# Two attentions and two layers of experts in one kernel: row buffers of the first experts, their places, and the order of keys and values

## The reference

```python
x = x + tanh(g_xattn[0]) * attention0(layernorm(x), ctx, ctx)     # 16 heads of 16, 128 keys per batch
x = x + tanh(g_ffn[0])   * experts0(layernorm(x))                 # 8 experts, top 2 of each token, 256 -> 1024 -> 256, exact GELU
x = x + tanh(g_xattn[1]) * attention1(layernorm(x), ctx, ctx, bias)
x = x + tanh(g_ffn[1])   * slots_and_experts1(layernorm(x))       # 16 slots, 16 experts with SiLU gates, attention back
```

## Time and profile before

| | us |
|---|---|
| median of 3 runs | 1462.82 (1461.97 to 1466.13) |
| the profiled execution | 1461.18 |
| its span, first to last instruction | 1459.4 |
| granted TensorE clock, mean | 0.978 |
| busy: PE, DVE, ScalarE, POOL | 1359.3, 928.2, 759.3, 381.4 |

### The profile page before, as it was taken

How to read it: one execution, slowest core, us unless ns; L and a number is a source line. 1 busy time by engine, 2 the same in 40 slices (tenths; PEclk the granted TensorE clock), 3 DMA queues, 4 the chain that set the end, 5 groups by cost and what they waited for, 6 DMA issues and landing times.

```text
span 1459.4 us, 39417 instructions
## 1 busy us (share of the span) xinstructions
PE 1359.3 (93%) x14238; PEld 1167.0 (80%) x14238; DVE 928.2 (64%) x2579; ACT 759.3 (52%) x1731; POOL 381.4 (26%) x478
## 2 busy tenths in 40 slices
PE   6999999995889999999999996999999999899798
PEld 5888888884779898989889995889989898645476
DVE  4789999886445455545445544788888887412187
ACT  3666666652545455555455552555656655332344
POOL 0244444443011303021321004433433431100131
PEclk9999999998899999999999997999999999999999
DMA  4665445454121212121221102631111110299911
GB/s 158 240 239 171 150 160 171 154 182 155 63 88 37 95 44 96 37 95 47 85 95 40 42 30 69 220 130 45 47 59 46 45 52 13 115 388 429 352 53 66
DMA packets 94567, 175.18 MB, mean 120 GB/s; under 512 B 9008, under 2 KB 84784, under 8 KB 89904
## 3 DMA queue, kind: packets, MB, share of 16 engines
q1 hardware_dynamic: 87376, 143.30, 27.4%
q0 software_dynamic: 7008, 29.37, 5.8%
HBM read 112.87 MB, written 59.77 MB: 118 GB/s over the span
## 4 chain that ended last, share of the span: by engine, by line
PE 74%; DVE 14%; DMA 7%; issue 3%; ACT 2%; POOL 0%; SPq 0%; DVEq 0%; ACTq 0%; PEldq 0%; POOLq 0%
PE ps L1222 13%; PE ps L1207 6%; PE psS L511 4%; DMA arena<-xs_rows 4%; PE psS L1207 4%; PE ps L663 3%; PE psT L1207 3%; PE ps L554 3%; PE psT L520 3%; PE ps L558 3%; DVE arena L879 3%; PE ps L618 2%; PE ps L603 2%; PE ps L630 2%; PE ps L1194 2%
## 5 line engine op out<-in xcount | busy, mean ns | idle before, releaser
L520 PE MATMUL psT<-arena 32*128 32x128 f32 x2048 | 148.8, 283 | 0.1
L511 PE MATMUL psS<-arena 32*128 32x256 f32 x1024 | 140.3, 392 | 0.7 <-ACT arena L756 0.7
L1253 ACT ACTIVATE arena<-arena 128x512 f32<-128x512 f32 x142 | 89.7, 632 | 96.1 <-DVE arena L1279 96.1
L1222 PE MATMUL ps<-ring_hi,hT_hi 128*128 x568 | 139.1, 283 | 0.5 <-ACT hT_hi L1235 0.5
L1222 PE MATMUL ps<-ring_lo,hT_hi 128*128 x568 | 139.3, 283 | 0.0
L1298 DVE TENSOR_TENSOR arena<-ps,arena 128x256 f32<-128x256 f32 x71 | 30.2, 425 | 152.9 <-PE ps L1222 152.9
L520 PEld LDWEIGHTS psT<-arena 32*128 32x128 f32 x2048 | 124.3, 186 | 1.2 <-issue 1.2
L1222 PEld LDWEIGHTS ps<-ring_hi,hT_hi 128*128 128x128 f32 x568 | 108.6, 191 | 3.5 <-issue 0.7
L1222 PEld LDWEIGHTS ps<-ring_lo,hT_hi 128*128 128x128 f32 x568 | 108.8, 192 | 2.8
L879 DVE TENSOR_REDUCE arena<-psS 128x8 f32<-128x1024 f32 x64 | 78.4, 1225 | 47.4 <-PE psS L511 47.4
L1235 ACT CAST hT_hi<-psT 128x512 fp32r<-128x512 f32 x71 | 41.7, 587 | 127.0 <-PE psT L1194 126.9
(11 more groups left out here) (288 smaller groups left out, 3720.1 us busy)
## 6 DMA issues: line engine op xcount, KB each, us to landing
arena<-wset_dram SPq DMA_DIRECT2D x24, 2048.0 KB, 15.2
xs_rows<-arena SPq DMA_DIRECT2D x32, 1024.0 KB, 5.7
arena<-w_dram POOLq DMA_DIRECT2D x6, 2048.0 KB, 9.0
arena<-xs_rows SPq DMA_DIRECT2D x71, 128.0 KB, 2.0
ys_rows<-arena SPq DMA_DIRECT2D x71, 128.0 KB, 1.7
arena<-ctxT_dram SPq DMA_DIRECT2D x64, 128.0 KB, 2.2
x_all<-x_dram SPq DMA_DIRECT2D x32, 128.0 KB, 2.1
arena<-w_dram SPq DMA_DIRECT2D x2, 2048.0 KB, 11.7
```

What stands on the lines that cost most here:

```text
L511: last = nc.tensor.matmul(psS[:, b, c * D:(c + 1) * D], qT[p, k % 3, c, :], kbd[p, k % 3, c, :, :], start=A, stop=A or c == 1, skip_group_ ...
L520: nc.tensor.matmul(psT[:, b, j * P:(j + 1) * P], kbd[p, (k - 1) % 3, c, par, :], qT[p, (k - 1) % 3, c, :], start=j == 0, stop=False, skip_ ...
L1222: last = nc.tensor.matmul(ps[5][:, 0:D], hp[:, f, :], wp[:, bass.ds(ring[j - 1], 1), o:o + D], start=n == 0 and f == 0 and wp is ring_hi, ...
L1253: nc.scalar.activation(v, v, ACT.Gelu).then_inc(ge_a.sem, 1)
```

## The change

1. `xs`, the buffers of a unit's rows, become four (`XS`), and lie in the first two weights of layer 0, which are dead by then but for the small product `prep`; SP issues `rows_in(j + 4)` where it issued `rows_in(j + 2)`. A unit's output is stored to the rows of `xs_dram` that it came from, through a second read of `unit_s`; `ys_dram` is gone, and so is the table of places. Units beyond the last real one get seven spare blocks, zeroed at the start of the kernel. The scatter's index is kept for the later gather, one column for each batch.
2. The weights of the two experts are made by `weights(dve, j)` in iterations 3, 4 and 5, in front of the wait for the unit's last product.
3. Unit 0 is always expert 0's first block; its rows are loaded before the unit table is there. PE starts a unit's products when the high part is there, waits for the low part in front of the third pair, and transposes unit 1 between the halves of unit 0, into bank 5. b1 is loaded in two halves. `prep` uses banks 6 and 7, and its DVE part comes one step later.
4. Attention 0 makes keys and values of batch 0 ahead of the steps (banks 6 and 7), of batches 1 and 2 behind the queries of batch 0 (banks 3 and 2). Attention 1 makes those of batches 0 to 4 ahead of the steps (banks 6, 7, 3, 2, 4), with two more context buffers and two more of `kbd` and `vz`. SP loads the contexts 2 and 3 during `moe0`, and 4 and 5 at the head of attention 1; its steps load a context only from batch 6 on.
5. ScalarE runs one exponential of one column at the head of each attention, which brings its table.

```diff
+XS = 4
-ROWS_EACH = TOKENS + P
+ROWS_EACH = TOKENS
+SPARE = E0 - 1
...
+        xs = w_sb[:, 0:2].rearrange("p n c d -> p (n c d)").rearrange("p (n d) -> p n d", n=XS)
...
             def sync(sp):
+                for i in () if A else (4, 5):
+                    sp.wait_ge(kv_p.sem, kv_p.at(i - 4, "V"))
+                    sp.dma_start(ctxT[:, i % 2].rearrange("p c t -> p (c t)"), a["ctxT"][i]).then_inc(ld_ctx[i % 2], 16)
                 for k in steps:
...
+                    if not A and k == 2 + EARLY_SETS:
+                        sp.wait_ge(av_p.sem, av_p.at(4, "av"))
                     if not A and 3 <= k < 3 + EARLY_SETS:
                         sp.dma_start(set_at(k - 3).rearrange("p e f -> p (e f)"), a["wset"][k - 3]).then_inc(ld_set[k - 3], 16)
...
-                    if valid(k + 3) and k + 3 >= 2:
+                    if valid(k + 3) and k + 3 >= (2 if A else 6):
                         i = k + 3
-                        before(sp, pre_p.sem, pre_p.at(k + 1, "V"))
+                        before(sp, kv_p.sem, kv_p.at(k + 1, "V"))
                         sp.dma_start(ctxT[:, i % 2].rearrange("p c t -> p (c t)"), a["ctxT"][i]).then_inc(ld_ctx[i % 2], 16)
...
                 if A:
                     pe.wait_ge(ld_first, 32)
                     pe.wait_ge(ld_kv, 16)
+                    keys(0, 6)
+                    values(0, 7)
                 else:
                     pe.wait_ge(ld_w, 16)
+                    for i in range(early):
+                        keys(i, early_bank[i])
+                        values(i, early_bank[i])
...
-                    if valid(k + 1):
-                        pe.wait_ge(ld_ctx[(k + 1) % 2], dma_at(k + 1, (k + 1) % 2))
+                    if valid(k + 1) and k + 1 >= early:
                         before(pe, m_a.sem, m_a.at(k - 1, "mT"))
                         before(pe, pre_a.sem, pre_a.at(k, "Q"))
...
+                        keys(k + 1, 6)
+                        values(k + 1, 6)
...
+                    if A and k == -1:
+                        for i in range(1, early):
+                            keys(i, early_bank[i])
+                            values(i, early_bank[i])
...
             def scalar(act):
...
                 if A:
+                    act.wait_ge(setup_v, 2)
+                    nc.scalar.activation(table[:, :], ones[:, 0:1], ACT.Exp)
                     act.wait_ge(setup_v, 3)
+                    act.wait_ge(kv_p.sem, kv_p.at(0, "K"))
+                    keys(0, 6)
+                else:
+                    nc.scalar.activation(table[:, :], ones[:, 0:1], ACT.Exp)
+                    for i in range(early - 1):
+                        act.wait_ge(kv_p.sem, kv_p.at(i, "V"))
+                        keys(i, early_bank[i])
+                        values(i, early_bank[i])
...
-                        before(dve, scat[sl_i % 2], dma_at(sl_i - 2, sl_i % 2, 2) if valid(sl_i - 2) else 0)
-                        nc.vector.tensor_copy(idx_put[:, sl_i % 2, :], slot_f[:, :, sl_i]).then_inc(rk_v.sem, 1)
+                        nc.vector.tensor_copy(slot_i[:, :, sl_i], slot_f[:, :]).then_inc(rk_v.sem, 1)
...
-                    if A and k == B + 2:
+                    if A and k == B + 3:
                         dve.wait_ge(prep_p, 1)
...
-                sp.wait_ge(route_v.sem, route_v.at(0, "unit_e"))
                 for s in scat:
                     sp.wait_ge(s, 16 * B)
                 sp.wait_ge(zero_dump, 16)
-                rows_in(0)
-                rows_in(1)
+                sp.wait_ge(prep_p, 1)
+                sp.dma_start(xs[:, 0, :], xs_dram[0:P, :]).then_inc(ld_xs[0], 16)
+                sp.wait_ge(route_v.sem, route_v.at(0, "unit_e"))
+                sp.wait_ge(prep_p, 3)
+                for j in range(1, XS):
+                    rows_in(j)
+                sp.dma_start(b1_sb[:, E0 // 2:].rearrange("p e f -> p (e f)"), a["b1"][:, E0 // 2 * F0:].partition_broadcast(P))\
+                    .then_inc(ld_b1[1], 16)
                 sp.dma_start(b2_sb.rearrange("p e d -> p (e d)"), a["b2"].partition_broadcast(P)).then_inc(ld_b2, 16)
+                for i in range(2):
+                    sp.dma_start(ctx_more[:, i].rearrange("p c t -> p (c t)"), a["ctxT"][2 + i]).then_inc(ld_more, 16)
                 for j in range(UNITS + 1):
-                    if ok(j + 2):
+                    if ok(j + XS):
                         sp.wait_ge(x_p.sem, x_p.at(j, "x"))
-                        rows_in(j + 2)
+                        rows_in(j + XS)
...
-                        sp.dma_start(ys_dram[(j - 1) * P:j * P, :], yb[:, (j - 1) % 2, :]).then_inc(st_ys[(j - 1) % 2], 16)
+                        sp.dma_start(xs_dram[bass.ds(first_row(j - 1), P), :], yb[:, (j - 1) % 2, :]).then_inc(st_ys[(j - 1) % 2], 16)
...
-                        pe.wait_ge(x_v.sem, x_v.at(j, "lo"))
+                        pe.wait_ge(x_a.sem, x_a.at(j, "hi"))
                         pe.wait_ge(ring_ready, e + 1)
                         for h in range(2):
                             before(pe, b1_v.sem, b1_v.at(j - 2, f"h{h}"))
+                            if j == 0 and h == 1:
+                                turned(1)
                             for n, (xp, wp) in enumerate(((xT_hi, ring_hi), (xT_hi, ring_lo), (xT_lo, ring_hi))):
+                                if n == 2 and h == 0:
+                                    pe.wait_ge(x_v.sem, x_v.at(j, "lo"))
...
+                    weights(dve, j)
                     if ok(j - 1):
                         dve.wait_ge(dn_p.sem, dn_p.at(j - 1, "y"))
...
-                    if j == 3:
-                        slots_and_weights(dve)
...
-                sp.dma_start(xs_dram[DUMP:DUMP + P, :], zero[:, :]).then_inc(zero_dump, 16)
+                sp.dma_start(xs_dram[DUMP:, :].rearrange("(n p) d -> p n d", p=P),
+                             zero[:, None, :].to_broadcast([P, SPARE, D])).then_inc(zero_dump, 16)
```

219 lines of the change are left out of this document (122 added, 97 removed).

## The result

The change makes the kernel faster, by 1.7% and less than I forecast: **1439.58 us** in the median of four runs (1435.5 to 1442.45), beside 1463.1 for the kernel before; the ratio is 0.9834, 95% interval [0.9804, 0.9864]. The forecast was 1428.5, its range ended at 1438.0. The direction was right, the range missed by 1.6 us. The profiled execution of the changed kernel took 1442.45 us (span 1440.6), so its rows stand for the slow end of those runs.

A forecast was written before the change was run, and what follows sets the result against it. The prediction took TensorE (PE) to bound the kernel, busy for 1359.3 of 1459.4 us. Its terms, -25.3 - 4.2 - 5.1 - 2.4 + 2.7 = -34.3, gave 1426.9 on the profiled execution and 1428.5 us on the median; range 1418 to 1438.

The forecast's parts named there:

- Four buffers, and rows written back: Experts of layer 0: four row buffers remove six stalls, -25.3 us; dropping the table of places gives -4.2 us.
- Start of attention 1: Five key and value pairs ahead, but gathers delayed by a 2 MB weight set: +2.7 us, bounds -6 and +8.
- first maximum 894.8 + 6.1 = 900.9, in place of 894.78: Start of attention 1: late gathers put the first query transposes at 894.8, and the first maximum 6.1 us later.
- 0.5 of slow Q against 1.5 won: Attention 1, steps 0 to 3: losing their pairs wins 1.5 us, slow query matmuls cost 0.5.
- this meeting: Start of attention 1: SP's 2 MB set meets the gathers; batch 0's second gather lands at 891.6, in place of 885.5.
- Start of attention 0: Table load moved, copy not waiting for values, keys and values of batches 1 and 2 ahead: -2.4 us, bounds 0 and -5.
- That eats the lead. It comes back in steps 0 and 1: Attention 0: pairs ahead use up Q's earlier start; step 1 without its pair wins 1.1 us, 0.7 behind Q(1), 0.6 next Q.
- Entry of the experts: From attention 0 to unit 0's last GELU: earlier scatter, rows and products, -5.1 us, bounds -3.7 and -5.8.
- the last scatter starts some 2.5 us earlier: Entry of the experts: own index buffer removes a 1.32 us wait, small product behind the last ranking gives 1.2 us.
- the second (1433.8 to 1438): Rival at attention 1, chance 0.08: two sets in a row also delay batches 1 and 2, clock low another step.
- The fourth: Rival in the experts, chance 0.02: SP becomes the bound, slower than before; 1463 at 7.2 us a unit, 1477 at 7.4.
- the third: Rival in the experts, chance 0.07: stalls stay despite early row loads; half staying gives 1441, all 1454.

The follow-up runs named there:

- e3_xs2: The changed kernel with two buffers for the rows in place of four; median 1472.3 us, ratio to the kernel before 1.0066.
- e7_busy: e6_prep_behind with matmuls nobody reads in PE's gaps at the starts of both attentions and ahead of unit 0's transposes; median 1424.4 us.
- e1_zero_late: The changed kernel with the zeroing of the seven spare blocks moved from the setup to step 10 of attention 0; 1434.91 us, ratio to before 0.9796.
- e4_kv_in_steps: e1_zero_late with keys and values of batches 1 and 2 of attention 0 back in their steps; median 1433.38 us.
- e9_late_steps: The changed kernel with late zeroing, late layer 1 weight sets, and attention 0's batches 1 and 2 keys and values in their steps; 1427.05 us, ratio 0.975.
- e10_busy_seam: e9_late_steps with matmuls nobody reads in PE's gaps from attention 0's last steps into unit 0, and at attention 1's start; 1419.52 us, ratio 0.9692.
- e6_prep_behind: The changed kernel with late zeroing, late layer 1 weight sets, and the small product's matmuls behind the last ranking product; median 1429.6 us.
- e11_before_again: The kernel before, unchanged, run and profiled once more; median 1464.7 us.
- e0_again: The changed kernel, without further edits, run and profiled once more; median 1442.6 us.
- e2_set_late: The changed kernel with SP waiting for the previous step's first maximum ahead of each of layer 1's four weight sets; median 1436.7 us.

## Why the prediction came out as it did

**Four buffers, and rows written back: -29.5, right.** 29.6 measured, 462.25 us from unit 0 to unit 69; e3_xs2 splits it into 23.6 for the buffers, where the sum had 25.3, and 6.0, where it had 4.2. What was sound is the 6.70 us of an undisturbed unit: all profiles with four buffers have 462.2 to 462.3. That the difference came out to a tenth is in part luck of the one execution of before: from unit 0 to unit 69 its repeat took 494.1 us, and 31.9 would be won against that.

**Start of attention 1: +2.7 forecast, +5.5 measured; the mechanism right, the size 2.8 short.** SP's set comes with the gathers, as the working has it; E grew by 6.2, as the step "first maximum 894.8 + 6.1 = 900.9, in place of 894.78" says. Two errors cancel in it: the second gather was issued 0.6 later behind the last y than I had it (5.15 us, 859.76 - 854.61, in place of 4.56), and landed in 7.4 us in place of 8.0. The shorter step 0 came too: the second maximum stands 25.6 us behind the last y (880.17 - 854.61), in place of 21.5 (900.58 - 879.04), so 4.0 later, where I had 3.7. The term that failed is the last one, "0.5 of slow Q against 1.5 won": from the second maximum to the first of step 5 nothing was won, and 1.5 lost (41.5 in place of 40.0). The clock stayed at the lower level until about 891, 11 us behind the second maximum; before, it rose at about that maximum. With the clock at full (e7_busy) F falls by 4.5, where here it fell by 0.7. Here the row of before that I cited against the Trainium skill, page "DMA: Bandwidth & Descriptors", section "Queues, rings and completion order", was the better guide: by the page's alternation of queues packet by packet the gathers would hardly have been held up. They land in 7.4 to 7.6 us beside the set, and the second is used 2.8 us after its issue without it. At like clock this meeting is worth the 3 to 3.7 us named above.

**Start of attention 0: -2.4 forecast, +3.3 measured.** Two things failed. The working never counted the zeroing, which grew from one block to seven (128 to 896 KB) and stands on SP's queue in front of context 2, which the pairs ahead want at 13.7 (16.44 - 2.77), where its step used to want it only behind the first scores of step 1, at 29.67: e1_zero_late takes 3.7 us off, some 3 of them at like clock. And "That eats the lead. It comes back in steps 0 and 1" failed twice. At the full clock no gain of the pairs ahead is seen (42.1 and 42.2, e7_busy and e4_kv_in_steps). And the clock was taken for granted: with the pairs ahead it fell in every profile that has no added matmuls, and was low for 14 to 24 us, where with the pairs in their steps it was low for 0, 0 and 6.8 (e4_kv_in_steps, e9_late_steps, e10_busy_seam); A grows by about 0.4 us for each microsecond of that (42 to 48.3 over 17.1 us with the late zeroing). What does bring time is the table load and the earlier copy: in e4_kv_in_steps Q starts at 10.8, 3.4 us earlier than before, 0.8 of which is an earlier first matmul (6.12 in place of 6.92); the other 2.6 is what I had. The other 2.9 of that run's 6.3 us go with the clock, which is full there from about 12 us on; in the kernel before the blocks up to 22.7 us took the longer of two durations (keys 2.08 us in place of 1.16, scores 2.08 in place of 1.13).

**Entry of the experts: -5.1 forecast, +0.6 measured.** Behind the last cast it went as worked out: 6.73 us from there to unit 0's transposes (370.66 - 363.93), in place of 8.34, and 8.98 from these to the end of the last GELU (378.49 + 1.15), in place of 10.40 (375.33 + 0.63 - 365.56). The step that failed is "the last scatter starts some 2.5 us earlier". It had 1.3 us for the index buffer and 1.2 for the small product. The second was a misreading of the change: the product's matmuls stay in front of the last ranking, only DVE's part of it moves, and e6_prep_behind, which moves them, wins nothing. The first assumed that PE's and DVE's path to the last place keeps its length, but the clock fell 11 us behind the last first maximum, not 24, and the cast came 2.2 us later, not 2.5 earlier. Compared with the fall 17 to 19 us behind that maximum, the cast stands 32.4 behind it before (e11_before_again) and 31.0 to 31.2 after (e1_zero_late, e4_kv_in_steps, e9_late_steps), so the 1.3 is there, and the seam takes 57.7 and 53.2 to 53.5: 4.3 us won, near the forecast's 5.1 less 1.2.

Compared at like time at the lower clock the gain is smaller: 56.1 and 53.2 with 23.9 us of it (before, e4_kv_in_steps), 57.7 and 56.8 with 30.7 (e11_before_again, e3_xs2). So the change is worth 1 to 4 us at this seam, and the runs don't say it closer. The profiles with the early fall (after, e0_again, e2_set_late) have 56.7 to 56.8. Of the 3.3 us between after and e1_zero_late half lies ahead of the cast (32.9 beside 31.2) and half behind the last GELU, where after has a second dip of the clock (0.58 and 0.56 in the two stretches of 2 us from 379.1), 8.2 us to the y beside 6.6. That the falls ate the gain is read from these groups of profiles, not from a run that moves the fall alone; e10_busy_seam removes it, but has matmuls of its own on the path. e3_xs2 has a late fall and the second dip, and 56.8: the moment of the fall alone doesn't give the length. What sets the moment of the fall stays open.

**Sum.** On the profiled execution, start of attention 0, B, entry, attention 1 and G: 1426.9 + 5.7 + 1.2 + 5.7 + 2.8 + 0.2 = 1442.5, against 1442.45. The 1.2 is B, in all profiles of the changed kernels but e7_busy (2.3): 0.3 at step 22 and 1.0 at step 26, where PE waits once for a DVE instruction (line 919) of 0.96 us that otherwise takes 0.42. What lengthens it was not looked into. Of the rivals, the second (1433.8 to 1438) came nearest, though for its clock, not for batch 2. The fourth and the third didn't happen. The range was too narrow since it held no term for the clock: at one seam, executions with the same order of work there differ by up to 4 us (A, 49.6 to 53.6).

## What to carry to other kernels

Take a stall's price from the interval of its steps, as was done for the experts: the undisturbed interval gave the time after the change to 0.1 us, where prices of starts and ends, summed from single instructions, were off by 3 to 6. For a change at the seams, list every transfer whose issue moves or grows, also those in the setup, and ask which small load stands behind it: two held back here gave 3.7 and 5.9 us, of which some 3 each at like clock. Work moved in front of a wait doesn't only fill it; see in which windows the granted clock is then lost, and give that term both ends. And before one profile is compared with another, compare their time at the lower clock in the stretch: two orders of work are told apart only where it is alike.

## What the runs showed of the hardware that I had not expected

The same instructions in the same order can keep PE's full clock in one execution and lose it in the next (A 41.8 and 45.0), and the time of a kernel's runs follows the mean granted clock: e6_prep_behind took 1423.0, 1424.9, 1434.4 and 1434.8 us at 0.983, 0.982, 0.974 and 0.973. No long pause is needed for a fall: in e1_zero_late the longest idle stretch of PE in the ten microseconds ahead was 0.96. In A a microsecond at the lower clock cost about 0.4 us: 42 without any, 45.0 with 6.8, 48.3 with 17.1. Matmuls without a reader in the gaps raised the mean to between 0.994 and 0.999 and were worth 7.5 us (e9_late_steps to e10_busy_seam), though PE is the busiest engine of the kernel.

The granted clock of a window can also read 1.00 while PE runs slowly: in the kernel before, the eight matmuls of Q at 14.18 took 2.08 us in a window marked 1.00, and 1.16 at 10.75 after. The durations of a known block are the better sign there.
